# Second attention: the eight gathers of a batch issued one at a time between GpSimd's other work

## What is computed

```
x = norm(x + attention_16_heads_of_64(x))      # banded: key j < i + 64
x = norm(x + experts(x))                       # each token: 4 of 16 experts, weighted sum
x = norm(x + attention_16_heads_of_8(x))       # "second attention", full softmax over 256 keys
x = norm(x + gated_scan_output(x))             # a state c carried over the batches
```

## Time and profile before

| | |
|---|---|
| median of 3 runs | 1427.92 us (1427.06 to 1428.64) |
| span of the profiled execution | 1445.1 us, 36685 instructions |
| TensorE, VectorE, ScalarE, GpSimd busy | 88%, 70%, 64%, 53% |
| third stage | from 988.9 us to the end |

### The profile page before, as it was taken

How to read it: one execution, slowest core, us unless ns; L and a number is a source line. 1 busy time by engine, 2 the same in 40 slices (tenths; PEclk the granted TensorE clock), 3 DMA queues, 4 the chain that set the end, 5 groups by cost and what they waited for, 6 DMA issues and landing times.

```text
span 1445.1 us, 36685 instructions
## 1 busy us (share of the span) xinstructions
PE 1272.4 (88%) x9756; PEld 971.6 (67%) x9756; DVE 1014.5 (70%) x3763; ACT 931.4 (64%) x2825; POOL 770.7 (53%) x981
## 2 busy tenths in 40 slices
PE   7999999999999999984899998996787788788973
PEld 3777776777777777764899998993455455455652
DVE  2677777777777777775677776766787677678835
ACT  5878777777777778772465665653565555556644
POOL 1557777777777777775222121235466666664132
PEclk9999999999999999997899999997899989999997
DMA  9612222221112222221222223222323223222102
GB/s 340 206 60 74 73 73 73 73 73 54 47 51 72 69 71 71 73 74 58 62 71 82 77 82 90 81 79 65 80 58 78 67 53 85 58 61 64 36 1 59
DMA packets 149016, 110.98 MB, mean 77 GB/s; under 512 B 12833, under 2 KB 137249, under 8 KB 148770
## 3 DMA queue, kind: packets, MB, share of 16 engines
q1 hardware_dynamic: 139842, 92.45, 22.0%
q0 software_dynamic: 8192, 16.79, 4.1%
q10 hardware_dynamic: 864, 0.39, 0.1%
HBM read 47.27 MB, written 61.93 MB: 76 GB/s over the span
## 4 chain that ended last, share of the span: by engine, by line
PE 60%; DVE 10%; issue 8%; ACT 7%; another core or an unknown queue 4%; DMA 3%; SPq 3%; DVEq 3%; ACTq 1%; POOL 0%; POOLq 0%
PE psum L911 9%; PE psum L922 8%; PE psum L798 6%; PE psum L835 6%; PE psum L853 5%; PE psum L746 4%; PE psum L815 3%; PE psum L753 3%; PE psum L947 3%; PE psum L747 3%; ACT wall L1183 2%; PE psum L935 2%; PE psum L1018 2%; ACT P L1153 2%
## 5 line engine op out<-in xcount | busy, mean ns | idle before, releaser
L554 POOL TENSOR_SCALAR P<-P,rinv 128x192 f32<-128x192 f32 (+1 forms) x384 | 308.5, 816 | 158.7 <-DVE rinv L1335 151.7
L1153 ACT ACTIVATE P<-shifted,least 128x192 f32<-128x192 f32 (+1 forms) x512 | 240.2, 470 | 100.6 <-DVE least L1321 99.1
L1175 ACT ACTIVATE hid<-psum,wA 128x128 f32<-128x128 f32 x576 | 164.4, 368 | 123.8 <-PE psum L911 120.2
L1512 DVE TENSOR_REDUCE mx<-psum 128x2 f32<-128x512 f32 x256 | 165.2, 687 | 66.4 <-PE psum L1018 42.3
L1321 DVE CUSTOM_DVE_ANT_0 shifted<-psum,band 128x192 f32<-128x192 f32 (+1 forms) x512 | 168.9, 385 | 27.5 <-PE psum L798 27.2
L598 POOL DMA_INDIRECT yk<-xs,posc x128 | 125.6, 981 | 107.4 <-DVE wA L1473 57.6
L1183 ACT ACTIVATE wall<-psum 128x1024 f32<-128x1024 f32 x128 | 130.8, 1022 | 65.7 <-PE psum L935 47.5
L911 PE MATMUL psum<-xgT,wA 128*128 128x128 f32 x1152 | 156.0, 279 | 2.0 <-ACT hid L1175 1.4
L922 PE MATMUL psum<-wB,hid 128*128 128x128 f32 x1152 | 152.6, 276 | 0.0
L911 PEld LDWEIGHTS psum<-xgT,wA 128*128 128x128 f32 x1152 | 143.3, 195 | 3.2 <-ACT hid L1175 1.8
L835 PEld LDWEIGHTS psum<-ident,P 128*128 128x128 f32 x1024 | 117.6, 141 | 35.8 <-issue 29.4
(11 more groups left out here) (261 smaller groups left out, 2537.0 us busy)
## 6 DMA issues: line engine op xcount, KB each, us to landing
xs<-zrow SPq DMA_DIRECT2D x34, 1024.0 KB
xg<-xs SPq DMA_DIRECT2D x144, 64.0 KB, 1.8
xs<-yrow SPq DMA_DIRECT2D x144, 64.0 KB
wall<-in_wall SPq DMA_DIRECT2D x1, 8232.0 KB, 36.3
qkd<-parts SPq DMA_DIRECT2D x64, 96.0 KB
kst<-qkd SPq DMA_DIRECT2D x22, 128.0 KB
qst<-qkd SPq DMA_DIRECT2D x22, 128.0 KB
wall<-qkd SPq DMA_DIRECT2D x20, 128.0 KB
```

The lines of the kernel that those rows point to most:

```text
L554: g.tensor_scalar(x, x, rinv[:, par, n:n + 1], None, ALU.mult).then_inc(s["pn_ready"], 1)
L1153: last = sc.activation(P[:, par, it, h, 0:w], shifted[:, par, it, h, 0:w], ACT.Exp, scale=-1.0, bias=least[:, par, n:n + 1], accum_out=row ...
L1175: sc.activation(hid[:, n % 4, f, :], up(n, f), ACT.Gelu, bias=wA[:, n % 4, F + f:F + f + 1]).then_inc(s["hid_ready"], 1)
L1512: v.tensor_reduce(out=mx[:, :, h], in_=SB[(par + 1 + h) % 3].rearrange("q (i n) -> q i n", i=TT), axis=mybir.AxisListType.X, op=ALU.max).t ...
```

## The change

`combine` and `new_state` are cut in two pieces each, and the two calls `fetch(b, par, 0)` and `fetch(b, par, 1)` are replaced by eight calls that issue one gather each, in the same order of gathers. The copy of the positions stays in front of gathers 0 and 4. Gather 1 waits in addition until eleven heads of the iteration have their maxima (in p = 5), and gather 7 until six heads of the next iteration have theirs (end of its p = 2). The first `drain()` of `combine` now stands behind gather 3, and the one ahead of the state's last operation behind gather 5.

```diff
--- before.py
+++ after.py
@@ -622,40 +622,60 @@
                     g.tensor_tensor(x_all[:, bass.ds((b + 3) * TT, TT), :], x2c[:, :, :],
                                     bo1[:, :].rearrange("q (o d) -> q o d", o=1).to_broadcast([128, TT, D]), ALU.add).then_inc(s["x2_kept"], 1)
 
-            def combine(b, par):
+            def combine(b, par, step):
 
                 if has(b, 4):
-                    need_alone(pool, "weighed", 2 * (b + 5))
                     y4 = yk[:, (par + 1) % 3, :, :].rearrange("q (i k) d -> q i k d", i=TT)
-                    g.tensor_tensor(y4[:, :, 0:2, :], y4[:, :, 0:2, :], y4[:, :, 2:4, :], ALU.add)
-                    g.drain()
-                    g.tensor_tensor(acc, y4[:, :, 0, :], y4[:, :, 1, :], ALU.add)
-                    g.drain()
-                    g.tensor_tensor(acc, acc, x_all[:, bass.ds((b + 4) * TT, TT), :], ALU.add).then_inc(s["comb_done"], 1)
-
-            def new_state(b):
+                    if step == 0:
+                        need_alone(pool, "weighed", 2 * (b + 5))
+                        g.tensor_tensor(y4[:, :, 0:2, :], y4[:, :, 0:2, :], y4[:, :, 2:4, :], ALU.add)
+                    if step == 1:
+                        g.drain()
+                        g.tensor_tensor(acc, y4[:, :, 0, :], y4[:, :, 1, :], ALU.add)
+                        g.drain()
+                        g.tensor_tensor(acc, acc, x_all[:, bass.ds((b + 4) * TT, TT), :], ALU.add).then_inc(s["comb_done"], 1)
+
+            def new_state(b, step):
 
                 if has(b, -2) and not (isinstance(b, int) and b >= B):
-                    need_alone(pool, "gate_act", b - 1)
-                    g.tensor_scalar(tf[:, :], tf[:, :], 1.0, 0.5, ALU.add, ALU.mult)
-                    g.tensor_scalar(ti[:, :], ti[:, :], 1.0, None, ALU.add)
-                    g.drain()
-                    g.tensor_tensor(c2[:, :], c2[:, :], tf[:, :], ALU.mult)
-                    g.tensor_tensor(tg[:, :], tg[:, :], ti[:, :], ALU.mult)
-                    g.drain()
-                    g.tensor_tensor(c2[:, :], c2[:, :], tg[:, :], ALU.add).then_inc(s["scan_done"], 1)
-                if has(b, -2):
+                    if step == 0:
+                        need_alone(pool, "gate_act", b - 1)
+                        g.tensor_scalar(tf[:, :], tf[:, :], 1.0, 0.5, ALU.add, ALU.mult)
+                        g.tensor_scalar(ti[:, :], ti[:, :], 1.0, None, ALU.add)
+                        g.drain()
+                        g.tensor_tensor(c2[:, :], c2[:, :], tf[:, :], ALU.mult)
+                        g.tensor_tensor(tg[:, :], tg[:, :], ti[:, :], ALU.mult)
+                    if step == 1:
+                        g.drain()
+                        g.tensor_tensor(c2[:, :], c2[:, :], tg[:, :], ALU.add).then_inc(s["scan_done"], 1)
+                if has(b, -2) and step == 1:
                     need_alone(pool, f"free{GB[0]}", tally[GB[0]].before(b, GB[1] + 1))
                     xo = xo_all[:, bass.ds((b - 2) * TT, TT), :]
                     g.tensor_tensor(xo, xo, bo2[:, :].rearrange("q (o d) -> q o d", o=1).to_broadcast([128, TT, D]), ALU.add).then_inc(s["xo_kept"], 1)
 
+            def fetch_one(b, par, k, heads=None):
+
+                half, n = k // (TT * TOPK // 2), k % (TT * TOPK // 2)
+                if has(b, 5):
+                    if heads is not None:
+                        need_alone(pool, "max_done", H1 * (b + 1) + heads)
+                    fetch(b, par, half, n, n + 1)
+
             def outputs(b, par):
                 deviations(b)
-                fetch(b, par, 0)
+                fetch_one(b, par, 0)
+                fetch_one(b, par, 1, 11)
                 keep(b)
-                combine(b, par)
-                new_state(b)
-                fetch(b, par, 1)
+                fetch_one(b, par, 2)
+                combine(b, par, 0)
+                fetch_one(b, par, 3)
+                combine(b, par, 1)
+                fetch_one(b, par, 4)
+                new_state(b, 0)
+                fetch_one(b, par, 5)
+                new_state(b, 1)
+                fetch_one(b, par, 6)
+                fetch_one(b, par, 7, H1 + 6)
 
             def combine_ahead(b, n):
```

## The result

The change made the kernel slower: 1450.26 us median against 1428.28 us, ratio 1.0151 with a 95% interval of 1.0126 to 1.0175. I had forecast 1416.4 us, 0.8% faster, and a range that ended at 1436. One of the changed kernel's four runs took 1651.11 us at a granted clock of 0.737, is counted in its median and left out of the ratio; the three others lie between 1448.31 and 1451.21.

What follows compares the result with a forecast made beforehand. Runs of gathers were taken to stall the third stage; spread, GpSimd's chain would set 26.1 us a batch: 8 * (26.96 - 26.1) = 6.9, plus 4.6, is 11.5 us off 1427.9, giving 1416.4 us, range 1390 to 1436.

Steps and rivals of the forecast that it cites:

- The base: Third stage, b = 3 to 10: 26.96 us a batch, 5.2 more than without gathers, laid to runs of gathers.
- The 4.6 us that I added for b = -1 to 2: Third stage's first stretch: 1.9 us gained in each of three batches, 5.7, less 1.1 for b = 2.
- The support from the expert stage: Expert stage: a tile with a run's third gather took 3.73 us, tiles with a lone gather or none 1.89.
- The agreement of 5.8 us of waits with 5.2 us of pace: Middle stretch: ScalarE's unnamed waits, 5.8 us a batch, matched the 5.2 us that batches with gathers cost more.
- The drain: GpSimd's drains behind gathers 3 and 5 wait for landing: 2 * 2.3 = 4.6 us, replacing 0.93 and 0.14.
- GpSimd's chain: GpSimd's own work per batch in the middle stretch: 22.5 us before, 26.1 us with the change.
- this second chain: State update to TensorE's gates: update 6.4 us later, 3.9 after the weighing's wait goes; period can shrink 1.2, to 25.8.
- The cover: Between the state update's end and the next gates on TensorE: 5.1 us, read from b = 8.
- The waits on maxima: Added waits of gathers 1 and 7 on GpSimd: cost nothing, gather 1 being ready only about when its head is.
- The slower one: GpSimd's drain behind gather 3 meets late packets, 4.8 us; chain 28.6, slower from 27.5 on; 1436 us, chance 0.22.
- The third rival: Third stage: runs of gathers don't cause the stalls, chain of 26.1 hides below 26.96, time stays 1428; chance 0.10.
- What would show it: Signs: ScalarE's unnamed waits nearly gone, 2.3 us gaps at L634 and L650, TensorE and VectorE idle, period near 26.

Runs made afterwards that it cites:

- b_again: The kernel before, without an edit, profiled a second time: 1425.65 us, ratio 1.000.
- b_third: The kernel before, without an edit, profiled a third time: 1429.0 us in one run.
- e6: The kernel before with one more drain directly behind the eighth gather of every batch: 1440.55 us, ratio 1.0113.
- e7: The kernel before with gathers 2 and 3 moved behind the state update, in one run with gathers 4 to 7: 1420.73 us, ratio 0.9957.
- e2: The changed kernel with only gathers 0 to 3 spread; gathers 4 to 7 in one run behind the update as before: 1422.52 us, ratio 0.9980.
- e3: The changed kernel with only gathers 4 to 7 spread; gathers 0 to 3 in one run as before: 1434.57 us, ratio 1.0068.
- e1: The changed kernel with the two drains ahead of gathers 3 and 5 in place of behind them: 1438.63 us, ratio 1.0103.
- e5: The changed kernel with drains ahead of gathers 3 and 5 and without the two added waits on maxima: 1438.45 us, ratio 1.0084.
- e4: The changed kernel without the two added waits on maxima of gathers 1 and 7: 1447.06 us, ratio 1.0148.
- e8: The kernel before with all eight gathers of a batch in one run behind the state update: 1450.49 us, ratio 1.0143.

## Why the prediction was wrong

**The base.** The step that failed is the first: "So a batch with gathers costs 5.2 us more than one without", read together with ScalarE's unnamed waits as "a run of gathers holding up TensorE's results or their signals". The 26.96 us and the waits belonged to one execution, which I had seen to be 17.2 us above the median, and I laid the difference aside with "I take the same gain off the median". In ordinary executions the same runs of gathers have no such waits, and a batch takes 24.2 to 24.4. By the prediction's own sum, 8 * (24.2 - 26.1) = -15 us without a gain in the first stretch, the time would have come out near 1443, on the slower side and above the range. The 4.6 us that I added for b = -1 to 2 did not come either: that stretch takes 99.09 us against 99.18. The support from the expert stage (3.73 against 1.89) was from the same execution and so was no second witness.

The agreement of 5.8 us of waits with 5.2 us of pace was real, but for that execution only. The batches without gathers, 21.73 us each, take 22.9 in `b_again` and 21.8 in `b_third`.

**The drain.** "GpSimd's drain waits until its gathers have landed" is borne out by `e6`, packets included, and by the gaps at L634 and L650 with the change. I had 2.3 us for each behind a gather; measured were 15.9 / 8 = 1.99 and 16.1 / 8 = 2.01, besides 3.5 / 8 = 0.44 at the drain between, behind gather 4, which I had not counted. But I set 0.93 against them as the old price at L632; it is 15.5 / 8 = 1.94 in `b_again`, which already pays for the run of half 0, by GpSimd's waits there:

```profile
POOL sums L632 <- issue: 15.5, 8, 2.2
...
POOL rstd L612 <- DVE ve L94: 7.7, 9, 2.1
```

So the added drain time is nearer 2.2 us a batch than 3.6: (15.9 + 16.1 + 3.5 + 1.9 - 15.5 - 1.9 - 1.2 - 1.1) / 8.

**GpSimd's chain.** I said 26.1 us (22.5 - 1.07 + 4.6 is 26.0); the period became 27.2. GpSimd's own chain, without its waits for others, measures (217.81 - 13.2 - 6.1) / 8 = 24.8, shorter than I said, and still the period is longer. GpSimd's own program is not the only thing that closes the circle: deviations, combine, state update, gates on TensorE, next norms, next deviations. I had this second chain, with "6.4 us" by which the update moves and "3.9 are left" after the weighing's wait goes. There was no weighing wait to lose in the ordinary execution; the update ended 7.6 us later (24.16 against 16.54). Of these, 2.2 are the drains, about 2.8 the two gathers more (2 * 1.42), and (13.2 + 6.1) / 8 = 2.4 are waits for VectorE between deviations and keep, in the time that gathers 2 and 3 had filled. That last term I had put at nothing. The cover was 3.66 us and not 5.1, and the way from the gates to the next deviations gave back 1.1: 7.6 - 3.5 - 1.1 = 3.0 us more a batch, 24 us in eight. That is the result. TensorE's lower clock is inside it: once it waits for the update, the heads and norms that GpSimd waits for come later as well. How much of the 3.0 us that makes is open, since no run changes the clock alone; over the versions it goes roughly with the period, from 0.99 in `e7` and 0.98 in `b_again` over 0.95 (`e2`), 0.94 (`e3`, `e6`), 0.93 (`e1`) and 0.92 (`e5`) to 0.90 (changed, `e4`) and 0.88 (`e8`).

**The waits on maxima** were said to cost nothing. In place they took 13.2 us of GpSimd's time, but `e4` shows that without them the idle time moves to the keep; the time changed by 3 us, within the intervals. So the two waits as such cost little, as I said, but my reason was wrong: gather 1 does wait for its head, and GpSimd idles there or at the keep because the gathers that used to fill the time stand behind it.

**The rivals.** The slower one named the drain behind gather 3 and late packets, a chain of 27.5 as the point of decision, and 1436. Its sign came true and its mechanism in part: `e1` gives the two drains' place 11.6 of the 22 us. Spreading by itself is not what costs: `e2` spreads half 0 and is no slower. `e5` has neither the drains behind gathers 3 and 5 nor the waits on maxima, and is still 0.84% slower, with gathers 3, 4 and 5 between the start of combine and the update's end. I read the rest as the price of where the gathers stand; its drains still wait for gathers 2 and 4, so the two are not separated. The third rival, that the runs don't cause the stalls, was the right reading of that part, as far as eleven of the twelve profiles show. The Trainium skill, page SBUF — State Buffer, section Who interferes with whom, says that a DMA never contends with a compute engine. The eleven profiles agree with it, with 0 us of unnamed waits on ScalarE in the stretch; the first has 46.4 us, whose cause is not known. The rival's conclusion "the time stays 1428" took the chain of 26.1 to be hidden below 26.96, which was the wrong base again.

**What would show it**: the gaps of about 2 us at L634 and L650, no idle time ahead of the deviations and TensorE idle ahead of the gates all appeared; the unnamed waits were gone, but not because of the change. Two signs did not come: the period was 27.2 and not near 26, and VectorE had no idle time ahead of the refinement of the norms in the middle stretch.

## What to carry to other kernels

Before a trace is used for a sum, its span must be held against the timed runs; where it lies as far above them as here (1.2%), a second profile comes first, because waits without a releaser may belong to that execution alone. On GpSimd a drain counted here as a wait for the gathers in flight, so gathers go behind the last drain of a dependent chain, or into time in which the engine waits for another anyway (here between deviations and keep), and in neither case later than their reader needs them. An engine that looks half idle (53% here) can carry the chain that closes the loop: add up the way round, with its cover, before putting work into it.

## What the runs showed of the hardware

A drain of GpSimd directly behind a run of four indirect gathers held its program 4.1 us (37.3 us in nine, `e6`), and one behind a gather that came alone 2.0 us (1.99 and 2.01 with the change), though the gather's own record ends after 0.98 us. It ended 0.3 to 1.8 us behind the last packet of the gathers' queue (`b_again`, `e6`, `e7` and the changed kernel); with the packets over before it began it cost 0.5 (`e6`) to 0.8 us (`e8`). A run's last gather had its last packets 2.2 us behind its start while nothing else moved, and about 4 while other transfers did (`e6`, `b_again`). Behind 6.12 us of TensorE's idle time the granted clock was 0.50, and the gates' first two matmuls took 1.22 us together, against 0.70 at full clock. Gathers in runs of four, six and eight left no unnamed waits on the other engines. The execution of the first profile was 17.2 us longer than the median of its kernel, with 46.4 us of unnamed waits on ScalarE in a stretch of 216 us; its cause stays open.
